# A residual graph network: counting loop by single chunks, input loaded tile by tile, mixing table made first

## The chip, the cores and the metric

The kernel runs on one core of a Trainium2 chip. The time is the device time of one execution in microseconds (us). The core has five engines with a program each: TensorE (PE, matmuls; its weight loads are shown as PEld), VectorE (DVE), ScalarE (ACT), GpSimd (POOL) and SyncE (SP, which here only issues DMAs). They wait for each other through semaphores. SPq and ACTq in the profile are the DMA issues of SP and ACT.

## The reference, cut to what matters

```python
x   = normal(1250, 512)
src, dst = [s, d, loop], [d, s, loop]     # 10000 random pairs both ways and 1250 self loops: 21250 edges, sorted by dst
x = layernorm(x + L0(x))   # GCN convolution with W (512x512), batch norm, gelu, residual
x = layernorm(x + L1(x))   # two SAGE layers: relu(h @ W_self + mean_of_neighbours(h) @ W_neigh + b)
x = layernorm(x + L2(x))   # two relational layers, two relations, weights mixed from 30 bases:
                           #   w[r] = sum_b att[r, b] * basis[b]          (30 x 512 x 512)
                           #   msg  = sigmoid(x_j @ gate_w[r]) * x_j @ w[r], r = edge_type; summed by row
x = layernorm(x + L3(x))   # x + neighbours' sum, relu(x @ W1 + b1) @ W2 + b2
```

All four layers use the same edges. So the kernel first turns the edge list into a matrix of counts (how many edges of each relation go from node s to node d) and then computes every sum over neighbours as a matrix product with it.

## The kernel before, in words

The change lies in the first stage, the counting stage, which runs until about 206 us. Afterwards come seven units (`UNITS`), each with a dense product for ten tiles of 128 nodes (`dense`) and a product with the counts (`agg`); nothing of them is touched.

**Counting.** The edges, sorted by dst, lie in `CHUNKS` = 170 chunks of 128. The 1280 padded nodes are cut into `NWIN` = 40 windows of 32 destination nodes. For each chunk that a window touches, VectorE writes two one-hot tables: `oh_lo` (128 columns: the low part of src) and `oh_key` (640 columns: destination within the window, relation, and tile of src), by two instructions (L1130 and L1132). TensorE multiplies them (L568, two matmuls of 320 columns for each chunk) and adds them up in PSUM, one matmul group for each window. ScalarE copies the sum to `B` (`window_out`, L758). Four windows make a node tile: TensorE turns its counts by products with the identity (`turn_counts`, L589, five groups in `COUNT_STEPS`), ScalarE copies them to `A` (L764), VectorE adds the two relations into `AT` (`sum_counts`, L1155), and TensorE counts degrees (L597).

Which chunks a window touches is found on the chip: VectorE takes the smallest and largest dst of each chunk (L1076), compares them with the windows' limits (L1079 to L1088), GpSimd takes the maximum over partitions (L510), and VectorE packs for each window the first chunk, the number of extra loop turns and their running sum into `tbl` (L1109 to L1123). The window's work goes by pairs of chunks: two fixed pairs, and between them a loop (`Fori`) of `more` turns with a pair each. Every window takes at least `LEAST` = 3 pairs, so the loop has at least one turn, and an odd number of chunks is rounded up. The tables lie in rings: `2 * FIXED` pairs for the fixed ones and `MORE` = 2 pairs for the loop's. VectorE may begin window w when TensorE has finished window w-2 (`wait(dve, s_win, w - 1)`).

**Mixing.** Beside this TensorE mixes the first relational layer's weights: 8 groups of 15 products in fp32 (L612), `mixT` (a table made by VectorE from att, L1092 to L1095) times a tile of 256 KB of the bases. Each is one "mix", and takes two rows of matmul in the profile. SP loads the tiles into 8 slots (`load_mix`); tile n waits until mix n-8 is done (`s_mx` at n-7). 15 mixes come ahead of window 0, the other 105 are spread behind the windows, two or three behind each (`SHARES`), in the order window, turned counts, mixes. ScalarE writes out each finished group (`mixed_out`).

**The input.** SP loads x behind the first 15 basis tiles, in a DMA of 2 MB (tiles 0 to 7, L465) and two small ones (L466, L468). VectorE takes the largest magnitude of x in five pieces (L1262, L1265), one each in front of windows 6 to 9 and the last in front of window 10, followed there by the maximum of the first weights (`most`, L1193) and `sum_counts`. GpSimd spreads the maximum over the partitions; behind window 12 VectorE makes the scale (`s_s0`). ScalarE then splits x into two fp16 halves tile by tile (`split_x`, L795 and L797) behind windows 17, 19, ... 35, and GpSimd computes the low half (L542).

## Time and profile before

| | us |
|---|---|
| time before, median of 3 runs | 944.89 (941.42 to 945.36) |
| the profiled execution | 940.41 |
| its span | 938.4 |
| TensorE busy in the span | 893.2 |
| VectorE busy | 681.1 |
| ScalarE busy | 280.8 |
| GpSimd busy | 86.1 |
| window 0 starts on TensorE | 21.71 |
| window 39 starts on TensorE | 200.99 |

The profile is one execution. Its times count from the span's start. "Busy" is the time in which an engine has an instruction in work; matmuls overlap in their records, so the distance from one start to the next is the rate, and a single record is longer than that. What stands in square brackets behind a row is how long the engine had been idle and what released it; "issue" there is a time in which the engine waited for nothing that the profile shows. The DMA columns give the busy share of the 16 DMA engines and GB/s. A row that merges several instructions shows their count behind x and the time from the first start to the last end.

### The profile page before, as it was taken

The numbers are of one execution on the slowest core, as the hardware profiler recorded it, in microseconds if no ns is written. First come the engines' busy times: TensorE is split into PE (matmuls) and PEld (weight loads), VectorE is DVE, ScalarE is ACT, GpSimd is POOL, SyncE is SP. The second block draws the span as 40 slices with busy tenths as digits, with TensorE's granted clock in tenths as the row PEclk, the third lists the DMA queues.
The fourth block names the chain that finished last, engine by engine and source line by source line (L and its number), as shares of the span: only waits on it lengthen the run. The fifth ranks groups of instructions, "written<-read, shape, count | busy, mean of one in ns | idle before, by whom it ended". The sixth has DMA issues, their size and how long they took to land.

```text
span 938.4 us, 13110 instructions
## 1 busy us (share of the span) xinstructions
PE 893.2 (95%) x4320; PEld 433.9 (46%) x4320; DVE 681.1 (73%) x1469; ACT 280.8 (30%) x431; POOL 86.1 (9%) x66
## 2 busy tenths in 40 slices
PE   6798999999996999999999899999999999999997
PEld 3354555554554544434444344444444444444443
DVE  7598998866997789798999888995324245552247
ACT  0132444443863313324132211113411131032321
POOL 1000011120321001202121000001300010010000
PEclk9899999999997999999999899999999999999999
DMA  8855556559544585788643765450031014322238
GB/s 261 275 163 157 157 182 181 171 136 232 159 147 135 144 239 177 191 248 176 182 120 97 168 147 171 124 127 12 22 79 34 1 54 115 90 66 46 39 66 229
DMA packets 134779, 129.53 MB, mean 138 GB/s; under 512 B 80575, under 2 KB 81044, under 8 KB 134714
## 3 DMA queue, kind: packets, MB, share of 16 engines
q10 hardware_dynamic: 96192, 60.25, 25.2%
q1 hardware_dynamic: 38522, 68.45, 25.0%
q8 instruction: 36, 0.59, 0.3%
q14 instruction: 29, 0.24, 0.1%
HBM read 97.80 MB, written 12.52 MB: 118 GB/s over the span
## 4 chain that ended last, share of the span: by engine, by line
PE 64%; DVE 17%; DMA 7%; ACT 4%; issue 3%; DVEq 1%; ACTq 1%; POOL 1%
PE Dp L658 24%; PE Dp L688 24%; PE T L612 9%; PE Dp L568 5%; DVE acc L1239 4%; DVE Zraw L1350 1%; DMA xr<-xres 1%; DVE stt L1331 1%; ACT W L1002 1%; DMA wst<-mixd 1%; DVE w L1368 1%; ACT wst L853 1%; DMA Zraw<-in_basis 1%; DMA stage<-in_basis 1%; POOL Zraw L525 1%
## 5 line engine op out<-in xcount | busy, mean ns | idle before, releaser
L658 PE MATMUL Dp<-W,hT 128*128 128x512 f16 x792 | 175.7, 381 | 3.6 <-DMA hT<-S 3.6
L688 PE MATMUL Dp<-Zraw,A 128*128 128x512 f16 x800 | 173.0, 379 | 0.0
L1239 DVE SCALAR_TENSOR_TENSOR acc<-stage,att,acc 128x512 f32<-128x512 f32 x232 | 163.7, 770 | 3.2 <-DMA stage<-in_basis 3.1
L688 PE MATMUL Dp<-Zraw,AT 128*128 128x512 f16 x600 | 130.0, 379 | 0.0
L658 PEld LDWEIGHTS Dp<-W,hT 128*128 128x128 f16 x792 | 77.7, 98 | 96.7 <-DMA hT<-S 3.8
L688 PEld LDWEIGHTS Dp<-Zraw,A 128*128 128x128 f16 x800 | 78.3, 98 | 94.4
L1132 DVE TENSOR_SCALAR Zraw<-hT,w 128x640 f16<-128x640 f16 (+1 forms) x240 | 114.4, 476 | 0.6 <-issue 0.4
L688 PEld LDWEIGHTS Dp<-Zraw,AT 128*128 128x128 f16 x600 | 58.7, 98 | 70.8
L1130 DVE TENSOR_SCALAR Zraw<-hT,w 128x128 f16<-128x128 f16 (+1 forms) x240 | 62.6, 261 | 24.8 <-PE Dp L568 15.9
L568 PE MATMUL Dp<-Zraw 128*128 128x320 f16 (+1 forms) x480 | 73.4, 300 | 3.3 <-DVE Zraw L1132 2.8
L1368 DVE SCALAR_TENSOR_TENSOR w<-Dp,aggc,S 128x512 f32<-128x512 f32 x40 | 29.9, 747 | 60.0 <-PE Dp L688 54.0
L954 ACT ACTIVATE Zraw<-Dp,zsc 128x512 f16<-128x512 f32 x46 | 29.4, 684 | 126.3 <-PE Dp L658 122.9
L612 PE MATMUL T<-stage,W 128*128 128x512 f32 x120 | 60.4, 626 | 7.2 <-DVE W L1095 7.2
L568 PEld LDWEIGHTS Dp<-Zraw 128*128 128x128 f16 (+1 forms) x480 | 46.7, 98 | 44.2 <-issue 27.7
L612 PE MATMUL T<-Zraw,W 128*128 128x512 f32 x120 | 58.4, 609 | 6.6 <-DMA Zraw<-in_basis 6.6
L1308 DVE SCALAR_TENSOR_TENSOR Zraw<-Dp,zsc,Zraw 128x512 f16<-128x512 f32 x26 | 19.5, 749 | 59.0 <-ACT Zraw L954 59.0
L525 POOL TENSOR_TENSOR W<-wst,W 128x1024 f16<-128x1024 f32 x18 | 43.1, 2415 | 159.7 <-ACT W L856 159.7
L993 ACT ACTIVATE w<-w,s_in 128x512 f32<-128x512 f32 x30 | 21.6, 720 | 120.5 <-DVE w L1368 115.5
L758 ACT ACTIVATE Zraw<-Dp 128x640 f16<-128x640 f32 x40 | 28.1, 701 | 97.6 <-PE Dp L568 95.5
L658 PE MATMUL Dp<-W,stage 128*128 128x512 f16 x240 | 52.8, 379 | 1.2 <-DVE Zraw L1308 1.2
L713 PE MATMUL Dp<-AT,Zraw 128*128 128x512 f16 (+1 forms) x240 | 43.4, 344 | 0.0
L658 PE MATMUL Dp<-W,wst 128*128 128x512 f16 x144 | 34.0, 401 | 4.9 <-DVE S L1316 4.9
(174 smaller groups left out, 913.7 us busy)
## 6 DMA issues: line engine op xcount, KB each, us to landing
stage<-in_basis SPq DMA_DIRECT2D x180, 256.0 KB, 2.9
Zraw<-in_basis SPq DMA_DIRECT2D x60, 256.0 KB, 2.8
xres<-w ACTq DMA_DIRECT2D x30, 256.0 KB, 2.4
xr<-xres ACTq DMA_DIRECT2D x30, 256.0 KB, 2.9
wst<-in_Wn ACTq DMA_DIRECT2D x4, 1024.0 KB, 5.5
wst<-in_Ws ACTq DMA_DIRECT2D x4, 1024.0 KB, 5.6
wst<-mixd ACTq DMA_DIRECT2D x4, 1024.0 KB, 5.9
wst<-in_root ACTq DMA_DIRECT2D x3, 1024.0 KB, 6.8
```

What stands on the lines that cost most here:

```text
L525: pool.tensor_tensor(weights_of(u, m)[:, 1, 2 * h:2 * h + 2, :], source, weights_of(u, m)[:, 0, 2 * h:2 * h + 2, :], ALU.subtract).then_in ...
L568: last = nc.tensor.matmul(Dp[:, j, b, 0:HALF], oh_lo[:, ds(slot * (2 * P) + q * P, P)], oh_key[:, ds(slot * (2 * KEYS) + (q * KEYS + b * H ...
L612: nc.tensor.matmul(T[:, 1, :], mixT[:, b * P:(b + 1) * P], mix_in[n % MIX_SLOTS], start=(b == 0), stop=(b == PAIRS - 1)).then_inc(s_mx, 1)
L658: last = nc.tensor.matmul(dense_bank(u, t, m), turned[:, hp, k * P:(k + 1) * P], weights_of(u, m)[:, wp, k, :], start=(n == 0), stop=(n == ...
L688: last = nc.tensor.matmul(sum_bank(t), a[:, k, ds(t * P, P)], Z[:, r, h, k, :], start=(n == 0), stop=(n == count - 1))
L713: last = nc.tensor.matmul(Df[:, j, c:c + w], Z[:, 0, h, k, b * P:(b + 1) * P], AT[:, k, c:c + w], start=(k == 0 and h == 0), stop=(k == NT ...
L758: nc.scalar.activation(B[:, t % 2, :, :, a:a + WIN].rearrange("p s r (b d) -> p b (s r) d", b=2), Dp[:, w % 2, 0:2, 0:HALF].rearrange("p b ...
L954: nc.scalar.activation(Z[:, r, 0, ds(t, 1), :], dense_rows(u, t, r), ACT.Copy, scale=scale).then_inc(s_zhi[u], 1)
L1130: v.tensor_scalar(oh_lo[:, ds(slot * (2 * P) + q * P, P)], iota_n[:, 0:P], lo_f[:, ds(c + q, 1)], None, ALU.is_equal)
L1132: last = v.tensor_scalar(oh_key[:, ds(slot * (2 * KEYS) + q * KEYS, KEYS)], iota_n, wkey[:, w:w + 1], key_f[:, ds(c + q, 1)], ALU.add, ALU ...
L1239: last = v.scalar_tensor_tensor(part, stage[:, q, :], a, part, ALU.mult, ALU.add)
L1368: v.scalar_tensor_tensor(w1[:, j:j + 1, :], sum_bank(t).rearrange("p (a d) -> p a d", a=1), c, rest, ALU.mult, ALU.add).then_inc(s_pre[u], 1)
```

## The change

- **Loop by single chunks.** `LEAST` is now 5 chunks, and the loop between the fixed pairs takes one chunk each turn (`chunk_of` on VectorE, `chunk_product` on TensorE). A window takes as many chunks as it touches, at least five. The loop's ring holds `MORE` = 4 single chunks, the same memory as two pairs. The table of windows no longer rounds to even numbers.
- **Input tile by tile.** x is loaded in ten DMAs of one tile, each behind three basis tiles of mixing groups 1 and 2.
- **Maximum later.** VectorE waits for all of x in front of window 10; the pieces of the maximum stand in front of windows 10 to 14, the scale behind window 17, and ScalarE splits x behind windows 19, 21, ... 37.
- **Mixing table first.** The first part of `mixT` is made right behind the two reductions over dst, ahead of the range operations; the second part behind them.

```diff
@@ -18,8 +18,8 @@
-MORE = 2
-LEAST = 3
+MORE = 4
+LEAST = 2 * FIXED + 1
...
@@ -428,8 +428,8 @@
-        XS_FROM = 4
-        Z_SCALED = 40
+        XS_FROM = 19
+        Z_SCALED = 38
...
@@ -462,13 +462,19 @@
             sp.dma_start(typ_i, typ_t).then_inc(e_edge, 16)
             sp.dma_start(src_i, src_t).then_inc(e_edge, 16)
             load_mix(0, MIX_FIRST)
-            sp.dma_start(acc_x, x[0:XA * P, :].rearrange("(t p) d -> p t d", p=P)).then_inc(e_x, 16)
-            sp.dma_start(xr[:, 0, :], x[XA * P:(NT - 1) * P, :]).then_inc(e_x, 16)
-            sp.wait_ge(s_pad, 1)
-            sp.dma_start(xr[0:LAST, 1, :], x[(NT - 1) * P:N, :]).then_inc(e_x, 16)
+
+            def load_x(t):
+                rows = min(P, N - t * P)
+                if rows < P:
+                    sp.wait_ge(s_pad, 1)
+                sp.dma_start(x_in(t)[0:rows, :], x[t * P:t * P + rows, :]).then_inc(e_x, 16)
+
+            for t in range(NT):
+                load_mix(1 + t // 5, 3 * (t % 5), 3 * (t % 5) + 3)
+                load_x(t)
             for tile, vec in ((b0T, b0), (gamT, gamma), (betT, beta)):
                 sp.dma_start(tile[:, :], vec).then_inc(s_bn, 16)
-            for mix_group in range(1, GROUPS):
+            for mix_group in range(3, GROUPS):
                 load_mix(mix_group)
             sp.dma_start(att[:, :, :].rearrange("p r b -> p (r b)"),
                          att2.rearrange("(a r) b -> a (r b)", a=1).broadcast_to([P, REL * BASES])).then_inc(s_att, 16)
...
@@ -561,14 +567,17 @@
         @block.tensor
         def _(pe):
 
-            def pair_product(slot, j, start=False, stop=False):
-
-                for q in range(2):
-                    for b in range(2):
-                        last = nc.tensor.matmul(Dp[:, j, b, 0:HALF], oh_lo[:, ds(slot * (2 * P) + q * P, P)],
-                                                oh_key[:, ds(slot * (2 * KEYS) + (q * KEYS + b * HALF), HALF)],
-                                                start=start and q == 0, stop=stop and q == 1)
+            def chunk_product(slot, j, start=False, stop=False):
+
+                for b in range(2):
+                    last = nc.tensor.matmul(Dp[:, j, b, 0:HALF], oh_lo[:, ds(slot * P, P)],
+                                            oh_key[:, ds(slot * KEYS + b * HALF, HALF)], start=start, stop=stop)
                 return last
+
+            def pair_product(pair, j, start=False, stop=False):
+
+                chunk_product(2 * pair, j, start=start)
+                return chunk_product(2 * pair + 1, j, stop=stop)
 
             def window(w, j):
                 _, more, base = window_range(pe, w)
...
@@ -577,7 +586,7 @@
                 pair_product(FIXED * (w % 2), j, start=True)
                 with pe.Fori(0, more) as i:
                     pe.wait_ge(s_more, base + i + 1)
-                    pair_product(pe.snap(((base + i) & (MORE - 1)) + OH), j).then_inc(s_moreu, 1)
+                    chunk_product(pe.snap(((base + i) & (MORE - 1)) + 2 * OH), j).then_inc(s_moreu, 1)
                 pe.wait_ge(s_oh, FIXED * (w + 1))
                 pair_product(FIXED * (w % 2) + 1, j, stop=True).then_inc(s_win, 1)
 
...
@@ -783,8 +792,10 @@
                             turned_out(t - 1, g, count_bank(t - 1, g))
                     for g in range(groups_done(w - 1) if w else 1, groups_done(w)):
                         mixed_out(g)
-                    first = (t - XS_FROM) * 2 + i // 2
-                    if i % 2 and 0 <= first < NT:
+                    first, odd = divmod(w - XS_FROM, 2)
+                    if first == 0 and not odd:
+                        act.wait_ge(s_s0, 1)
+                    if not odd and 0 <= first < NT:
                         split_x(first)
                     if w == NWIN - 2:
                         turn_to(2, 0)
...
@@ -1075,7 +1084,19 @@
             dve.wait_ge(e_row, 16)
             v.tensor_reduce(mnx[0:HC, 0:2], dstr[0:HC, :, :], AX.X, ALU.min)
             link(v.tensor_reduce(mnx[0:HC, 2:4], dstr[0:HC, :, :], AX.X, ALU.max))
-            dve.wait_ge(s_const, 5)
+            dve.wait_ge(e_att, 32)
+            dve.wait_ge(s_const, 8)
+            v.tensor_tensor(eye, ident[:, 0:P // 2], ident[:, P // 2:P], ALU.add).then_inc(s_eye, 1)
+            dve.wait_ge(s_eye, 1)
+
+            def mix_table(a0, a1):
+
+                v.tensor_tensor(mixT[:, a0 * P // 2:a1 * P // 2].rearrange("p (a i) -> p a i", a=a1 - a0),
+                                eye.rearrange("p (a i) -> p a i", a=1).broadcast_to([P, a1 - a0, P // 2]),
+                                attp[:, a0:a1].rearrange("p (a i) -> p a i", i=1).broadcast_to([P, a1 - a0, P // 2]),
+                                ALU.mult).then_inc(s_mixT, 1)
+
+            mix_table(0, 2 * MIX_FIRST)
             for g in range(2):
                 link(v.tensor_scalar(fl[0:HC, 0:NWIN], wlo[0:HC, :], mnx[0:HC, 2 + g:3 + g], None, ALU.is_le))
                 link(v.scalar_tensor_tensor(fl[0:HC, NWIN:2 * NWIN], whi[0:HC, :], mnx[0:HC, g:g + 1],
...
@@ -1087,15 +1108,7 @@
-            dve.wait_ge(e_att, 32)
-            dve.wait_ge(s_const, 8)
-            v.tensor_tensor(eye, ident[:, 0:P // 2], ident[:, P // 2:P], ALU.add).then_inc(s_eye, 1)
-            dve.wait_ge(s_eye, 1)
-            for a0, a1 in ((0, 2 * MIX_FIRST), (2 * MIX_FIRST, BASES)):
-                v.tensor_tensor(mixT[:, a0 * P // 2:a1 * P // 2].rearrange("p (a i) -> p a i", a=a1 - a0),
-                                eye.rearrange("p (a i) -> p a i", a=1).broadcast_to([P, a1 - a0, P // 2]),
-                                attp[:, a0:a1].rearrange("p (a i) -> p a i", i=1).broadcast_to([P, a1 - a0, P // 2]),
-                                ALU.mult).then_inc(s_mixT, 1)
+            mix_table(2 * MIX_FIRST, BASES)
...
@@ -1107,11 +1120,9 @@
-            link(v.tensor_scalar(w_st, w_st, float(CHUNKS - 2 * LEAST), None, ALU.min))
+            link(v.tensor_scalar(w_st, w_st, float(CHUNKS - LEAST), None, ALU.min))
-            link(v.tensor_scalar(w_n, w_n, float(2 * LEAST), 1.0, ALU.max, ALU.add))
-            link(v.tensor_scalar(w_n, w_n, 0x1FE, None, ALU.bitwise_and))
-            link(v.tensor_scalar(w_p, w_n, 0.5, -float(FIXED), ALU.mult, ALU.add))
+            link(v.tensor_scalar(w_p, w_n, float(LEAST), -2.0 * FIXED, ALU.max, ALU.add))
...
@@ -1124,14 +1135,16 @@
+            def chunk_of(w, slot, c):
+                v.tensor_scalar(oh_lo[:, ds(slot * P, P)], iota_n[:, 0:P], lo_f[:, ds(c, 1)], None, ALU.is_equal)
+                return v.tensor_scalar(oh_key[:, ds(slot * KEYS, KEYS)], iota_n,
+                                       wkey[:, w:w + 1], key_f[:, ds(c, 1)], ALU.add, ALU.is_equal)
+            def pair_of(w, pair, c):
+                chunk_of(w, 2 * pair, c)
+                return chunk_of(w, 2 * pair + 1, c + 1)
...
@@ -1140,11 +1153,11 @@
                     wait(dve, s_win, w - 1)
                     pair_of(w, FIXED * (w % 2), first).then_inc(s_oh, 1)
                     with dve.Fori(0, more) as i:
-                        c = nc.s_assert_within(dve.snap(first + i * 2 + 2 * FIXED), 0, CHUNKS - 2,
+                        c = nc.s_assert_within(dve.snap(first + i + 2 * FIXED), 0, CHUNKS - 1,
                                                skip_runtime_bounds_check_because=ends)
                         n = dve.snap(base + i)
                         dve.wait_ge(s_moreu, n + 1)
-                        pair_of(w, dve.snap((n & (MORE - 1)) + OH), c).then_inc(s_more, 1)
+                        chunk_of(w, dve.snap((n & (MORE - 1)) + 2 * OH), c).then_inc(s_more, 1)
                     pair_of(w, FIXED * (w % 2) + 1, nc.s_assert_within(dve.snap(first + 2), 0, CHUNKS - 2,
                                                                        skip_runtime_bounds_check_because=ends)).then_inc(s_oh, 1)
 
...
@@ -1256,18 +1269,18 @@
             for u in (1, 3, 5):
                 v.memset(s_in[:, u:u + 1], LN_SCALE)
                 link(v.memset(i_in[:, u:u + 1], 1.0 / LN_SCALE))
-            windows_to(6)
-            dve.wait_ge(e_x, 48)
+            windows_to(10)
+            dve.wait_ge(e_x, 16 * NT)
             for piece in range(4):
                 v.tensor_reduce(xcol[:, piece:piece + 1], acc_x[:, 2 * piece:2 * piece + 2, :].rearrange("p t d -> p (t d)"), AX.X,
                                 ALU.max, apply_absolute_value=True).then_inc(s_xc, 1)
-                windows_to(7 + piece)
+                windows_to(11 + piece)
             v.tensor_reduce(xcol[:, 4:5], xr[:, :, :].rearrange("p a d -> p (a d)"), AX.X, ALU.max,
                             apply_absolute_value=True).then_inc(s_xc, 1)
             dve.wait_ge(s_xc, 5)
             v.tensor_reduce(xin[:, :], xcol[:, :], AX.X, ALU.max).then_inc(s_xin, 1)
             weight_work("counts", 0, 0)
-            windows_to(13)
+            windows_to(18)
             dve.wait_ge(s_xmax, 1)
             power_scale(s_in[:, 0:1], i_in[:, 0:1], xmax[:, :])
             v.nop().then_inc(s_s0, 1)
```

On VectorE, at the start of the program, these rows stand before (w and hT hold the small tables of ranges, W holds `mixT`):

```order
L1076 TENSOR_REDUCE w<-hT 85x2
L1077 TENSOR_REDUCE w<-hT 85x2
L1080 TENSOR_SCALAR hT<-hT,w 85x40
L1081 SCALAR_TENSOR_TENSOR hT<-hT,w 85x40
L1085 SCALAR_TENSOR_TENSOR w<-hT,w 85x40 x2
L1080 TENSOR_SCALAR hT<-hT,w 85x40
L1081 SCALAR_TENSOR_TENSOR hT<-hT,w 85x40
L1085 SCALAR_TENSOR_TENSOR w<-hT,w 85x40 x2
L1092 TENSOR_TENSOR hT<-ident 128x64
L1095 TENSOR_TENSOR W<-hT,sd_att 128x384
L1095 TENSOR_TENSOR W<-hT,sd_att 128x1536
```

and these after:

```order
L1085 TENSOR_REDUCE w<-hT 85x2
L1086 TENSOR_REDUCE w<-hT 85x2
L1089 TENSOR_TENSOR hT<-ident 128x64
L1094 TENSOR_TENSOR W<-hT,sd_att 128x384
L1101 TENSOR_SCALAR hT<-hT,w 85x40
L1102 SCALAR_TENSOR_TENSOR hT<-hT,w 85x40
L1106 SCALAR_TENSOR_TENSOR w<-hT,w 85x40 x2
L1101 TENSOR_SCALAR hT<-hT,w 85x40
L1102 SCALAR_TENSOR_TENSOR hT<-hT,w 85x40
L1106 SCALAR_TENSOR_TENSOR w<-hT,w 85x40 x2
L1094 TENSOR_TENSOR W<-hT,sd_att 128x1536
```

The table's first part (128x384, three mixes' worth) has moved ahead of the range operations; the larger second part stands behind them in both.

On SP, the queue that issues the loads, this is the place where x stands (stage and Zraw are the basis slots, acc and xr the tiles of x), as a difference:

```order
+L470 DMA acc<-in_x 128x512
+L458 DMA stage<-in_basis 128x512 x2
+L458 DMA Zraw<-in_basis 128x512
+L470 DMA acc<-in_x 128x512
 L458 DMA Zraw<-in_basis 128x512 x3
-L465 DMA acc<-in_x 128x8x512
-L466 DMA xr<-in_x 128x512
-L468 DMA xr<-in_x 98x512
-L470 DMA b0T<-in_b 128x4
-L470 DMA gamT<-in_gamma 128x4
-L470 DMA betT<-in_beta 128x4
+L470 DMA acc<-in_x 128x512
```

The three loads of x have left their place behind basis tile 14; a tile of x now follows three basis tiles each time, down to the last one behind basis tile 44.

## Rows read from the trace of the kernel before

**Rows 1.** The page: TensorE's busy time, share of the span, instructions.

```profile
PE   893.2 (95%) x4320; PEld 433.9 (46%) x4320; DVE 681.1 (73%) x1469; ACT 280.8 (30%) x431; POOL 86.1 (9%) x66
```

**Rows 2.** Busy time by stretch: stretch, its length, then each engine; clock; DMA.

```profile
5.00:15.00 10.00, 7.85 (x15) 3.57 (x16) 8.23 (x35) 0.00 (x0) 0.81 (x4) 1.00 0.95 310
92.00:190.00 98.00, 97.94 (x565) 56.71 (x566) 89.41 (x290) 45.61 (x76) 11.91 (x10) 1.00 0.59 177
```

**Rows 3.** Who waited for whom, first 300 us: total us, times, longest.

```profile
DVE Zraw L1130 <- PE Dp L568: 15.9, 8, 9.0
```

**Rows 4.** Timeline, first 17 us: start, duration, engine, line, operation, operands, idle before.

```profile
2.39 1.53 SPq L458 DMA_DIRECT2D stage<-in_basis  x3
...
4.07 0.24 DVE L1080 TENSOR_SCALAR hT<-hT,w 85x40 f32<-85x40 f32 x1
...
6.54 2.23 DVE L1095 TENSOR_TENSOR W<-hT,sd_att 128x384 f32<-128x384 f16 x2
...
7.15 5.28 PE L612 MATMUL T<-stage,W 128*128 128x512 f32 x8 [7.15 <-DVE W L1095]
...
16.90 0.26 DVE L1130 TENSOR_SCALAR Zraw<-hT,w 128x128 f16 x1 [0.43 <-issue]
```

**Rows 5.** DMAs: landing of basis tile 0; of tiles at 10-60 us; x issue.

```profile
DMA to landing us min/median/max: 3.0/3.0/3.0
...
DMA to landing us min/median/max: 2.7/3.0/12.1
...
15.41 0.43 SPq L465 DMA_DIRECT2D acc<-in_x  x1
```

**Rows 6.** Timeline of TensorE, windows 0, 1 and 3 with the mixes behind.

```profile
21.71 1.79 PE L568 MATMUL Dp<-Zraw 128*128 128x320 f16 x12
...
30.14 2.05 PE L612 MATMUL T<-Zraw,W 128*128 128x512 f32 x2 [6.64 <-DMA Zraw<-in_basis]
...
33.69 2.08 PE L568 MATMUL Dp<-Zraw 128*128 128x320 f16 x12
...
41.53 1.79 PE L568 MATMUL Dp<-Zraw 128*128 128x320 f16 x12
43.16 1.88 PE L612 MATMUL T<-Zraw,W 128*128 128x512 f32 x4
44.87 1.02 PE L612 MATMUL T<-stage,W 128*128 128x512 f32 x2
```

**Rows 7.** Timeline of TensorE: starts of windows 9, 10, 11, 13, 15, 17, 19.

```profile
66.08 1.79 PE L568 MATMUL Dp<-Zraw 128*128 128x320 f16 x12
72.38 0.70 PE L568 MATMUL Dp<-Zraw 128*128 128x320 f16 x4 [1.43 <-DVE Zraw L1132]
...
77.34 1.79 PE L568 MATMUL Dp<-Zraw 128*128 128x320 f16 x12
...
85.45 0.71 PE L568 MATMUL Dp<-Zraw 128*128 128x320 f16 x4
...
95.61 1.79 PE L568 MATMUL Dp<-Zraw 128*128 128x320 f16 x12
...
103.72 1.79 PE L568 MATMUL Dp<-Zraw 128*128 128x320 f16 x12
...
112.33 1.79 PE L568 MATMUL Dp<-Zraw 128*128 128x320 f16 x12
```

**Rows 8.** Timeline of VectorE: window 8, then the maxima and sums before window 10.

```profile
58.36 0.24 DVE L1130 TENSOR_SCALAR Zraw<-hT,w 128x128 f16<-128x128 f16 x1
...
61.47 1.21 DVE L1262 TENSOR_REDUCE xcol<-acc 128x1 f32<-128x1024 f32 x1
...
65.71 1.21 DVE L1265 TENSOR_REDUCE xcol<-xr 128x1 f32<-128x1024 f32 x1
...
69.41 0.82 DVE L1155 TENSOR_TENSOR AT<-Zraw 128x1280 f16<-128x1280 f16 x1
...
71.11 0.25 DVE L1130 TENSOR_SCALAR Zraw<-hT,w 128x128 f16<-128x128 f16 x1 [0.63 <-issue]
```

21 lines of the change are left out of this document (6 added, 15 removed).

## The prediction

> **What bounds the kernel now.** I began with the page: TensorE is busy for 95% of a span of 938.4 us [rows 1], so a change pays only where it shortens TensorE's row of work or fills a hole in it. The edit lies in the counting stage, so I next cut the span into stretches. From 92 to 190 us TensorE is busy for 97.94 of 98.00 us at a granted clock of 1.00, while VectorE has 89.41 and the DMA engines are 59% busy [rows 2]. In its steady part the counting stage is TensorE's. The waits agree: VectorE stood for 15.9 us behind TensorE, eight times [rows 3]. Then I read TensorE's timeline for what is not steady: its first matmul at 7.15 us [rows 4], one hole of 6.64 us at 30.14 us, put down to a basis tile's DMA [rows 6], and windows that last longer than others of their kind [rows 7].
>
> The stage ends for TensorE with window 39 (201 us) and its three mixes, near 206 us; everything later waits for these results, in an order that the diff leaves alone. So I price the edits on this stage and take the difference through to the end.
>
> **Prices.** A window of six chunks starts at 41.53 and the next work at 43.16 [rows 6]: 1.63 us for 12 matmuls, 0.272 us for a chunk. Two mixes take 44.87 - 43.16 = 1.71 us, 0.857 each; a mix counts as two matmuls in the rows. Windows 17 and 18 run without a wait, 103.72 to 112.33 [rows 7]: 8.61 us for two windows, five mixes, three turned groups and the degrees. Groups and degrees cost what is left, 8.61 - 2 x 1.63 - 5 x 0.857 = 1.07, so 0.53 for each window. On VectorE six chunks take 61.47 - 58.36 = 3.11 us, 0.52 each, and a maximum of two x tiles 1.2 us [rows 8].
>
> **1. One chunk per loop turn.** A window holds 21250/40 = 531 edges, 4.15 chunks of 128, so it touches five or six. Working the ranges out with the reference's own dst gives 31 windows of five and 9 of six; before, all 40 take six. That removes 31 chunks: 31 x 0.272 = 8.4 us of TensorE, all on the path. VectorE is rid of 31 x 0.52 = 16.1 us, off the path in the steady part. Nine windows go round the loop twice, which no window of before does. The loop's entry and exit lie inside the 1.63 us already, so I take the second turn at 0. Its other end: VectorE stood 0.43 us at its first entry into the loop (16.47 to 16.90) [rows 4], and nine of those on TensorE would be 3.9 us. Below nothing it can't go, since it only adds instructions.
>
> **2. The x load in pieces.** Before, 2.5 MB of x go in front of basis tile 15 [rows 5]. TensorE could mix tile 15 at 21.71 + 1.63 = 23.34 and be at window 1 two mixes later, at 25.06; it is there at 33.69 [rows 6]. Lost: 8.6 us. Now one x tile of 256 KB follows every three basis tiles, and tile 15 is issued when eight mixes are done, about 14 us. Windows with 2.5 mixes each then need 2.5 x 4/3 = 3.3 tiles in some 4.0 us, 0.85 MB or 213 GB/s, with the first weights (1 MB) on top for a while. The queue moved 310 GB/s at 5 to 15 us, with only tiles of this size and the edge lists in it [rows 2]. So the hole goes: -8.6 us. Its bound on the other side is under the rivals.
>
> Those 310 GB/s are 91% of what a 1 MB transfer gets in a table of the Trainium skill (DMA: Bandwidth & Descriptors, Measured): 341 GB/s, against 138 for 64 KB, with the advice to batch DMAs to 1 MiB or more. That rule speaks against cutting a 2 MB load into eight. By it x would need an estimated 2.5/0.138 = 18 us instead of 2.5/0.341 = 7.3, at worst 11 us more of queue time. The row bears it out little: small DMAs in a row overlap.
>
> **3. Mixing table first.** VectorE makes the table's first part after the eight range operations (4.07 to about 6.1 us), at 6.54, and TensorE starts at 7.15 [rows 4]. With the table right behind the two reductions VectorE comes to it at 4.07; a short first step and the 0.61 us from 6.54 to 7.15 bring that to about 4.9. But basis tile 0, issued at 2.39, lands 3.0 us later [rows 4, 5], at 5.4. So TensorE starts at 5.45: -1.7 us. The next tiles come at some 0.85 us each and are taken at 0.857. If they come late the gain is 0. The range operations, and with them the table of windows, come 0.8 us later, but TensorE is in its 15 mixes until 19.6 us; nothing waits.
>
> **4. The maximum taken later.** The waits of before first. Windows 9 and 10 start at 66.08 and 72.38, window 11 at 77.34: 11.26 us for a pair that takes 8.61 elsewhere (17 and 18 have the same groups and mixes); 2.65 us lost, because VectorE has 71.11 - 65.71 = 5.40 us of maxima and sums in front of window 10 [rows 7, 8]. Windows 13 and 14 take 95.61 - 85.45 = 10.16 instead of 8.61: 1.55 lost [rows 7]. These 4.2 us go.
>
> New waits take their place, and here the edit pays back a third. VectorE now waits for all ten x tiles in front of window 10. The tenth stands behind basis tile 44, which waits for the 37th mix; that mix ends with window 8, so just when window 9 starts (call it 0). Two issues of 0.43 us and 3.0 us of landing [rows 5]: 3.9. Then queued on VectorE: one maximum (1.2, to 5.1), sum_counts with the table load (71.11 - 69.41 = 1.70, to 6.8) [rows 8], and five chunks (2.6, to 9.4). TensorE's last pair of chunks takes 0.54 more, so it ends window 10 at 10.0. Undisturbed it would start window 10 at 4.5 (1.36 + 0.53 + 2.57) and end it at 5.8. Lost: 4.2 us. Window 11 has six chunks behind another maximum and ends 0.4 late. By window 13 VectorE and TensorE are level (VectorE has made it at 21.0, TensorE ends it at 21.7). In front of window 14 stands the same string of 5.40 us that stood before window 10, then five chunks: 21.0 + 5.4 + 2.6 = 29.0, TensorE ends it at 29.6, undisturbed 21.7 + 0.53 + 2.57 + 1.36 = 26.2. Lost: 3.4 us. New waits: 4.2 + 0.4 + 3.4 = 8.0 us. Their ends: 0, if VectorE had enough lead, and 16, if the last x tile lands 8 to 9 us later (the longest landing is 12.1 us [rows 5]).
>
> The split of x moves two windows later (17 to 35, now 19 to 37), two windows before TensorE needs its results; I take 0.
>
> **Sum.** -8.4 - 8.6 - 1.7 - 4.2 + 8.0 = -14.9 us. The profiled execution took 940.4 us, of which 938.4 are the span; it becomes 925.5. That execution lies under all three timed runs (941.42 to 945.36, median 944.89); from the median the sum gives 930.0. A small rest speaks for a little more gain: the two mixes behind the hole ran at a slower clock (2.05 us for one [rows 6]). I forecast **929 us**.
>
> **Rivals.**
> A. *The new waits don't arise.* The last x tile would have to be there when VectorE comes, or VectorE two windows ahead through both places. For it: VectorE has 16 us less to do. Against it: it can't be more than two windows ahead, and the DMA's place behind the 37th mix is fixed. Gain 14.9 + 8.0 = 22.9: 921 to 922 us.
> B. *The new waits are twice as long*, the last x tile landing late while weights and mixed results move too. For it: the 12.1 us landing. Loss 16 in place of 8.0, perhaps with 2 us from loop turns: 937 us.
> C. *The range doesn't fit or the gains are given back.* If VectorE, not TensorE, set the period, 31 chunks less on TensorE would bring nothing; [rows 2, 3] speak against it. Or the second turn costs 3.9 us and the start gains nothing: together with B about 943.
> D. *Slower: the basis tiles starve.* Eight slots are in flight, and every three basis tiles carry an x tile behind them. With a landing time L, 30 mixes need 30 x 4/3 x L/8 = 5L us if slots are always waited for. Where TensorE would need about 50 us for this stretch (window 0 to 11), the other gains are used up from 5L = 66, L = 13.2 us. At L = 15 it is 75 us: nine more than before, 954 us. One landing of 12.1 us is in the rows, with 2.5 MB in front; the median is 3.0 [rows 5].
>
> **Chances.** Forecast 0.66, A 0.14, B 0.13, C 0.05, D 0.02. A measurement of this kernel tells about 0.5% (4.7 us) from no change. Faster by more: the forecast, A and nearly all of B, 0.93; within it: most of C and a rest of B, 0.05; slower: D, 0.02. Range 918 to 938: it takes in A at 921, less 3 for the runs' spread, and B at 937. The forecast's own range is 924 to 934.
>
> **What would show it.** (1) 418 chunk matmuls instead of 480, at 1.36 us for most windows, and none of the nine longer windows more than 0.3 us over 1.63. (2) No hole behind window 0; window 1 starts near 22.8, and the granted clock is 1.00 from 20 to 40 us. (3) First matmul at 5.3 to 5.6 us. (4) VectorE waits for a DMA into the x tiles in front of window 10, TensorE then waits for VectorE by about 4 us, and again by 3 to 4 us in front of window 14. (5) The first dense matmul of unit 0 starts near 191, not 206, and all later distances are as before. It is wrong if TensorE has no waits at windows 10 and 14 (A), or waits for basis tiles between windows 1 and 9 (D), or if the stage gets shorter and a later one longer.

## The result and the profile after

The changed kernel takes 932.5 us in the median of 4 runs (930.7 to 935.52), the kernel before 943.15 in 4 runs beside it (940.66 to 945.36). The ratio is 0.9901 with a 95% interval of 0.9876 to 0.9926: faster, by 9.3 us by the ratio (7.0 to 11.7 by its interval) and 10.7 by the medians. The forecast was 929 us with a range of 918 to 938. The range held the time and the sign was right; the forecast gain of 14.9 us was about half again too large. The profiled execution of after took 935.5 us (span 933.7), the slowest of its four, so the 4.7 us between the two spans are less than the medians differ by. I account for the counting stage, which the edit changes.

The page of after, against [rows 1]:

```profile
PE 888.9 (95%) x4258; PEld 428.9 (46%) x4258; DVE 668.8 (72%) x1405; ACT 280.8 (30%) x431; POOL 85.5 (9%) x66
...
L573 PE MATMUL Dp<-Zraw 128*128 128x320 f16 (+1 forms) x418 | 67.1, 307 | 9.2 <-DVE Zraw L1141 9.1
```

TensorE lost the 62 matmuls of 31 chunks, and a wait of 9.1 us for VectorE stands where there were 2.8. The stretches, against [rows 2]; the third is the one that had the hole:

```profile
5.00:15.00 10.00, 9.08 (x15) 3.94 (x16) 9.09 (x36) 0.00 (x0) 0.81 (x4) 1.00 0.94 324
92.00:190.00 98.00, 96.63 (x544) 54.41 (x544) 84.00 (x262) 48.97 (x80) 13.32 (x11) 1.00 0.59 173
...
20.00:40.00 20.00, 20.00 (x90) 10.71 (x89) 15.75 (x60) 4.61 (x7) 0.00 (x0) 1.00 0.97 343
```

From 20 to 40 us TensorE is busy without a gap. From 92 to 190, where it had 0.06 us idle before, it has 1.37. The waits of the first 220 us, against [rows 3]:

```profile
DVE Zraw L1140 <- issue: 15.7, 37, 1.2
PE Dp L573 <- DVE Zraw L1141: 9.1, 6, 3.6
...
DVE xcol L1275 <- DMA xr<-in_x: 6.7, 1, 6.7
...
DVE Zraw L1140 <- PE Dp L573: 4.7, 6, 1.5
```

The balance has turned: VectorE waits 4.7 us for TensorE (15.9 before), TensorE 9.1 for VectorE. TensorE's timeline, against [rows 4, 6, 7] (the start, windows 0 to 2, then windows 9, 10, 11, 13, 14 and 15; the view ends within window 15, so its row counts 11 of the 12 matmuls):

```profile
5.92 6.58 PE L621 MATMUL T<-stage,W 128*128 128x512 f32 x8 [5.92 <-DMA stage<-in_basis]
12.34 3.60 PE L621 MATMUL T<-Zraw,W 128*128 128x512 f32 x8
...
21.78 1.52 PE L573 MATMUL Dp<-Zraw 128*128 128x320 f16 x10
...
24.86 1.52 PE L573 MATMUL Dp<-Zraw 128*128 128x320 f16 x10
...
28.79 1.52 PE L573 MATMUL Dp<-Zraw 128*128 128x320 f16 x10
...
55.06 1.52 PE L573 MATMUL Dp<-Zraw 128*128 128x320 f16 x10
...
63.25 2.93 PE L573 MATMUL Dp<-Zraw 128*128 128x320 f16 x10 [3.59 <-DVE Zraw L1141]
...
68.46 1.92 PE L573 MATMUL Dp<-Zraw 128*128 128x320 f16 x12
...
76.43 1.52 PE L573 MATMUL Dp<-Zraw 128*128 128x320 f16 x10
...
83.30 2.93 PE L573 MATMUL Dp<-Zraw 128*128 128x320 f16 x10 [2.27 <-DVE Zraw L1141]
...
88.61 1.66 PE L573 MATMUL Dp<-Zraw 128*128 128x320 f16 x11
```

The hole is gone (window 0 to window 1: 3.08 us, before 11.98). TensorE starts earlier, but its first eight matmuls last 6.42 us to the next group, and window 0 starts no earlier than before. Windows 10 and 14 start late, and their ten matmuls take 2.93 us instead of 1.52: TensorE gets chunks at VectorE's pace, and its own is slower behind the idle time (see step 4). VectorE in front of window 10, against [rows 8]:

```profile
59.13 1.22 DVE L1275 TENSOR_REDUCE xcol<-acc 128x1 f32<-128x1024 f32 x1 [6.72 <-DMA xr<-in_x]
60.27 0.82 DVE L1168 TENSOR_TENSOR AT<-Zraw 128x1280 f16<-128x1280 f16 x1
...
61.98 0.25 DVE L1140 TENSOR_SCALAR Zraw<-hT,w 128x128 f16<-128x128 f16 x1 [0.64 <-issue]
```

VectorE had been done since 52.4 us and stood 6.7 us for the last x tile; only then came the maximum, the sum of the counts (`sum_counts`) and the chunks. The first dense matmul of unit 0 comes at 197.88 us (before 206.37): the stage is 8.5 us shorter. By windows (start to start, after less before, each a sum of the timeline's distances):

| stretch | forecast | measured |
| --- | --- | --- |
| start to window 0 | -1.7 | +0.1 |
| window 0 (the hole, one chunk) | -8.9 | -8.9 |
| windows 1 to 8 | -1.9 | -2.2 |
| windows 9 to 14 | +2.4 | +4.0 |
| windows 15 to 37 | -4.4 | -2.3 |
| windows 38 and 39 | -0.5 | +0.8 |
| sum | -14.9 | -8.5 |

The 6.4 us that are missing lie in four places: the start 1.8 (most of it this one profile's, as the third experiment shows), windows 9 to 14 1.6, windows 15 to 37 2.0, the last two 1.3; windows 1 to 8 gave 0.3 more than forecast. After the stage the distances of the two profiles differ by 3.8 us (732.0 and 735.8). The gap of the profiles is no measure of the edit there: kernels whose code there is the same gave 732 to 739 us for this part.

### The profile page after: what moved, and what is told of

The parts are those of the page before. It is cut to its first block, busy times and chain, and to the rows that moved or that the text cites. A ratio compares the mean times of both kernels' runs of the same rounds, so it can differ in the third digit from the quotient of the medians.

```text
span 933.7 us, 12912 instructions
## 1 busy us (share of the span) xinstructions
PE 888.9 (95%) x4258; PEld 428.9 (46%) x4258; DVE 668.8 (72%) x1405; ACT 280.8 (30%) x431; POOL 85.5 (9%) x66
## 4 chain that ended last, share of the span: by engine, by line
PE 61%; DVE 18%; DMA 7%; issue 5%; ACT 4%; DVEq 3%; POOL 1%; ACTq 0%; SPq 0%
PE Dp L667 25%; PE Dp L697 24%; PE T L621 6%; DVE acc L1252 4%; DMA stage<-in_basis 3%; PE Dp L573 3%; DVE Zraw L1141 2%; DMA wst<-mixd 2%; DVE Zraw L1140 1%; DVE Zraw L1363 1%; ACT W L1011 1%; PE T L667 1%; DVEq L1140 1%; ACT wst L864 1%; DVE w L1381 1%
## 5 line engine op out<-in xcount | busy, mean ns | idle before, releaser
L1141 DVE TENSOR_SCALAR Zraw<-hT,w 128x640 f16<-128x640 f16 (+1 forms) x209 | 96.4, 461 | 0.8 <-issue 0.7
L573 PE MATMUL Dp<-Zraw 128*128 128x320 f16 (+1 forms) x418 | 67.1, 307 | 9.2 <-DVE Zraw L1141 9.1
L1140 DVE TENSOR_SCALAR Zraw<-hT,w 128x128 f16<-128x128 f16 (+1 forms) x209 | 59.3, 284 | 22.1 <-issue 15.7
L573 PEld LDWEIGHTS Dp<-Zraw 128*128 128x128 f16 (+1 forms) x418 | 40.5, 99 | 48.8 <-issue 30.1
L531 POOL TENSOR_TENSOR W<-wst,W 128x1024 f16<-128x1024 f32 x18 | 42.9, 2400 | 158.2 <-ACT W L867 158.2
L963 ACT ACTIVATE Zraw<-Dp 128x512 f16<-128x512 f32 x26 | 15.5, 596 | 74.9 <-PE Dp L667 72.3
```

The lines of the kernel that those rows point to most:

```text
L531: pool.tensor_tensor(weights_of(u, m)[:, 1, 2 * h:2 * h + 2, :], source, weights_of(u, m)[:, 0, 2 * h:2 * h + 2, :], ALU.subtract).then_in ...
L573: last = nc.tensor.matmul(Dp[:, j, b, 0:HALF], oh_lo[:, ds(slot * P, P)], oh_key[:, ds(slot * KEYS + b * HALF, HALF)], start=start, stop=stop)
L963: nc.scalar.activation(Z[:, r, 0, ds(t, 1), :], dense_rows(u, t, r), ACT.Copy, scale=scale).then_inc(s_zhi[u], 1)
L1140: v.tensor_scalar(oh_lo[:, ds(slot * P, P)], iota_n[:, 0:P], lo_f[:, ds(c, 1)], None, ALU.is_equal)
L1141: return v.tensor_scalar(oh_key[:, ds(slot * KEYS, KEYS)], iota_n, wkey[:, w:w + 1], key_f[:, ds(c, 1)], ALU.add, ALU.is_equal)
```

## The experiments

Twelve kernels ran. Each ratio is to the kernel before on the same chip (medians 941.5 to 942.2 us in the four series), with its 95% interval. "Stage" is from the start of window 0 to the first dense matmul of unit 0: 184.7 us before, 176.1 after.

**The three parts alone.** Each is the kernel before with one part of the diff: the loop of single chunks; x in pieces and its maxima later; the mixing table first.

> The kernel before with the single-chunk loop alone; x stays one 2 MB load, maxima in front of windows 6 to 10. Theory T1 (a loop turn with one chunk costs VectorE more than its 0.52 us: in the changed kernel a window of five chunks took VectorE 3.07 us instead of 2.6, one of six with two turns 4.3 to 4.7 instead of 3.31): VectorE's windows show the same 3.07 and 4.3 to 4.7 us here, TensorE still gains on 31 windows, and the time is 5 to 8 us below before. Rival T2 (the lost gain comes only from VectorE having lost its lead in front of window 10, the loop costs nothing): VectorE's windows are 2.8 and 3.3 us and the time is 8.4 us or more below before.

Measured: 937.3 us, 0.9954 (0.9931 to 0.9977); stage 178.8. VectorE's undisturbed windows are those of T1: 3.07 us for five chunks, 4.34 for six (window 11). The gain, 4.3 us by the ratio and 5.0 by the medians, lies at the lower end of T1's 5 to 8 or just under it, and T2's 8.4 is out.

> The kernel before with the tile-by-tile load of x, the later maxima and the later split alone. Both theories: the hole behind window 0 goes (8.6 us), the old waits at windows 10, 13 and 14 (4.2 us) go, new ones come in front of windows 10 and 14. T1: these are as long as in the changed kernel less what its loop adds, 8 to 9 us together, so the stage ends 3 to 5 us earlier than before. T2 (the lead is lost because x comes late): the same, and in addition later windows wait for VectorE as in the changed kernel (windows 18 to 24 and 39).

Measured: 944.0 us, 1.0027 (1.0005 to 1.0050); stage 183.7. The hole was gone and nothing was won; the stage is 1.0 us shorter, where the expectation had 3 to 5 for both theories, and none of the windows 18 to 24 lost anything, against T2. TensorE at window 10, and VectorE's wait, in this kernel:

```profile
65.70 3.64 PE L574 MATMUL Dp<-Zraw 128*128 128x320 f16 x12 [3.67 <-DVE Zraw L1138]
```

```profile
DVE xcol L1268 <- DMA xr<-in_x: 7.2, 1, 7.2
DVE Zraw L1136 <- PE Dp L574: 7.1, 8, 1.3
```

Windows 9 and 10 lost 6.9 us against their undisturbed 8.61, windows 13 and 14 4.3, where before the two places lost 4.2 in all; the last two windows took 1.0 longer. Together that is 8.0 of the 8.6 us of the hole.

> The kernel before with the mixing table first alone. Forecast of the prediction: first matmul 1.7 us earlier and window 0 as much earlier. Theory C (TensorE starts earlier but stays at the slow clock for longer, as in the changed kernel, where weight loads of the first mixes stood 0.85 us apart until 11.9 us instead of 10.2): first matmul near 5.9 us, window 0 at 21.4 to 21.8, no gain. Rival: the basis tiles come too late; then the weight loads have idle times put down to a DMA in front of them.

Measured: 941.5 us, 0.9997 (0.9979 to 1.0015). TensorE started at 5.51 us, window 0 at 21.33 (before 21.71).

```profile
5.51 6.54 PE L612 MATMUL T<-stage,W 128*128 128x512 f32 x8 [5.51 <-DVE W L1085]
11.89 3.60 PE L612 MATMUL T<-Zraw,W 128*128 128x512 f32 x8
```

A start 1.64 us earlier leaves 0.38 at the second group. The way from the first matmul to window 0 varies by itself, from 14.6 to 15.9 us. Over all profiles window 0 starts at 22.2 us in the mean where the table comes late (6 kernels, 21.71 to 22.87) and at 20.9 where it comes first (8 kernels, 20.14 to 21.78): 1.3 us, which is within this run's interval. The expectation's slower first matmuls are there; what they are is the last point of this document.

**Parts one and two together.**

> Parts 1 and 2 of the change (one chunk per loop turn; x in pieces with its maxima later), the mixing table where it was. Theory (part 2 pays only with part 1: the hole behind window 0 was also the time in which VectorE caught up, and part 1 makes VectorE's windows 0.24 us shorter): about as the changed kernel plus the 0 to 1 us of the earlier start, 932 to 935 us. Rival (the parts add: ratios 0.9954 and 1.0027 alone): 0.998 of the kernel before, 940 to 942 us; then the third part would carry the difference.

Measured: 935.3 us, 0.9922 (0.9893 to 0.9952). The parts do not add: 0.9954 x 1.0027 would be 0.998, outside the interval. In the counting stage they nearly do: 5.9 and 1.0 us alone, 8.4 together (stage 176.3). The rest of the difference lies behind the stage, where no part changes the code, and no run tells why. The third part stands for the rest, 2.8 us by the medians, with intervals that overlap.

**Every window with two loop turns.** The changed kernel with the least number of chunks raised by one, so that 31 windows get back a sixth chunk, now as a second turn:

```diff
-LEAST = 2 * FIXED + 1
+LEAST = 2 * FIXED + 2
```

> The changed kernel with LEAST = 6 chunks: every window takes six chunks and two loop turns, as many chunks as before. T1: VectorE needs 4.3 to 4.7 us for each window and 1.7 more for every fourth, about 4.8 a window against TensorE's 4.4, so VectorE sets the counting stage: TensorE waits for it in most windows and the stage is 15 to 25 us longer than in the changed kernel, longer than before. T2: only the 8.4 us of TensorE's 31 chunks come back, the time is near 941.

Measured: 964.6 us, 1.0248 (1.0229 to 1.0267). The waits of the stage:

```profile
DVE Zraw L1140 <- issue: 27.4, 57, 1.2
PE Dp L573 <- DVE Zraw L1141: 19.9, 26, 3.0
```

31 more chunks cost 32 us where TensorE needs 0.27 each, 8.4 in all. The stage is 30.5 us longer than in the changed kernel, more than T1's 15 to 25. Windows 38 and 39 alone take 16.98 us in place of 10.84, since GpSimd holds VectorE up there (last section); the rest of the stage takes 24.3 us more, 0.8 for each of its 29 new chunks. TensorE waits 26 times, but not everywhere: windows 24, 27 and 28, for instance, take the 4.48 us that they took before. The price is in the changed kernel's own rows, VectorE's window 5:

```profile
34.13 0.25 DVE L1140 TENSOR_SCALAR Zraw<-hT,w 128x128 f16<-128x128 f16 x1 [0.16 <-issue]
...
35.30 0.25 DVE L1140 TENSOR_SCALAR Zraw<-hT,w 128x128 f16 x1
35.50 0.45 DVE L1141 TENSOR_SCALAR Zraw<-hT,w 128x640 f16 x1
36.57 0.25 DVE L1140 TENSOR_SCALAR Zraw<-hT,w 128x128 f16 x1 [0.62 <-issue]
```

From the first turn's chunk to the second's are 1.27 us, not 0.52. Without other work and waits a window of six chunks takes 4.33 us on VectorE (window 15), of five 3.07, and before, with two chunks in one turn, six took 3.31.

**The x load earlier.** The changed kernel with an x tile behind every two basis tiles:

```diff
-                load_mix(1 + t // 5, 3 * (t % 5), 3 * (t % 5) + 3)
+                for n in (2 * t, 2 * t + 1):
+                    load_mix(1 + n // PAIRS, n % PAIRS, n % PAIRS + 1)
                 load_x(t)
...
+            load_mix(2, 5)
```

> The changed kernel, but one x tile follows every two basis tiles instead of every three, so the tenth stands behind basis tile 19 (which waits for the 12th mix) and not behind tile 44 (the 37th mix). Theory (VectorE has no lead to spare, and what is put in its way is lost on TensorE): VectorE's wait of 6.7 us for the last x tile goes; without it the maximum starts near 52.4 us instead of 59.1 and the chunks of window 10 are ready before TensorE comes, so the 5.3 us lost at windows 9 and 10 go; VectorE reaches windows 13 and 14 with two windows of lead, and of the 4.1 us lost there 1 to 4 go too. Stage 6 to 9 us shorter: 924 to 927 us. Rival (only the late transfer matters): windows 9 and 10 lose nothing, windows 13 and 14 lose their 4.1 us as before: 927 to 928 us. Second rival (VectorE's whole work sets the stage, the place of the transfer does not matter; the waits come back further on): 931 to 933 us, as the changed kernel.

The expectation names a wrong place: the tiles are counted from tile 15 on, so the tenth x tile stands behind basis tile 34, which waits for the 27th mix, and was issued at 38.81 us (after: 55.63). Measured: 925.8 us, 0.9828 (0.9787 to 0.9869), the best version by the medians; stage 169.3. TensorE's windows 9, 10 and 11, and the wait in window 14:

```profile
54.16 1.52 PE L575 MATMUL Dp<-Zraw 128*128 128x320 f16 x10
58.59 1.52 PE L575 MATMUL Dp<-Zraw 128*128 128x320 f16 x10
62.23 1.79 PE L575 MATMUL Dp<-Zraw 128*128 128x320 f16 x12
...
75.59 0.70 PE L575 MATMUL Dp<-Zraw 128*128 128x320 f16 x4 [0.92 <-DVE Zraw L1143]
```

Windows 9 and 10 take 8.07 us, undisturbed, where the changed kernel needs 13.40; windows 13 and 14 take 10.03 in place of 12.18 (8.08 undisturbed). The theory's 924 to 927 held. The first rival falls by the windows (13 and 14 did not lose their 4.1 us again), the second by the time: the wait for the last tile was worth 5.3 us at window 10, and 2.2 us at window 14 by the lead that VectorE keeps.

**The x load early and the maxima earlier.** As the last one, with the maxima at windows 6 to 10 and the weights' maximum behind window 16:

```diff
-            windows_to(10)
+            windows_to(6)
             dve.wait_ge(e_x, 16 * NT)
...
-                windows_to(11 + piece)
+                windows_to(7 + piece)
...
+            windows_to(17)
             weight_work("counts", 0, 0)
```

> The changed kernel with the x tiles behind every two basis tiles, the five maxima of x in front of windows 6 to 10 instead of 10 to 14, and the maximum of the first weights (2.3 us) in front of window 17 by itself. In windows 1 to 9 TensorE has 2.5 mixes in each (4.0 us) where VectorE needs 3.07, so a maximum of 1.2 us fits there nearly for nothing. Theory (no lead): the 5.3 us at windows 9 and 10 and the 4.1 us at 13 and 14 both go, and windows 16 to 18 lose at most 1 us: 922 to 925 us. Rival (what counts is the sum of VectorE's work in the stage, wherever it stands): 930 to 933 us.

Measured: 934.5 us, 0.9914 (0.9887 to 0.9941): 8 to 9 us worse than the last, and my 922 to 925 was wrong. The rival's 930 to 933 is nearer to the number, but does not have the cause. By the misplaced tile above x was not there yet; the wait and most of the loss moved with the maximum (windows 5 and 6 lost 8.3 us, and windows 17 and 18, behind the weights' maximum, 2.9), here VectorE, then TensorE at window 6:

```profile
43.88 1.22 DVE L1277 TENSOR_REDUCE xcol<-acc 128x1 f32<-128x1024 f32 x1 [6.92 <-DMA xr<-in_x]
```

```profile
48.02 2.93 PE L575 MATMUL Dp<-Zraw 128*128 128x320 f16 x10 [5.33 <-DVE Zraw L1143]
```

The same two edits (x tiles, maxima) on the kernel before with part two:

> The kernel before (two chunks per loop turn) with part 2 alone, but with the x tiles behind every two basis tiles, the maxima in front of windows 6 to 10 and the weights' maximum in front of window 17. Part 2 alone gave 944.0 us against 942.2: it filled the hole of 6.6 us and lost as much at windows 9, 10, 13, 14 and 39. Theory (it was lost to VectorE's wait for the last x tile and to the two strings of its other work): most of the 8.6 us of the hole now shows: 935 to 938 us. Rival (VectorE's work of six chunks a window, 3.11 us, leaves no room without the hole, wherever the maxima stand): 941 to 944 us.

Measured: 943.1 us, 0.9996 (0.9972 to 1.0021), with the same wait of 6.9 us. It can't tell the two theories apart, since x came late in it; the next one does.

**Part two alone with x earlier,** the maxima at windows 10 to 14:

> The kernel before (two chunks per loop turn) with part 2, but an x tile behind every two basis tiles, so that the tenth stands behind basis tile 34 (it waits for the 27th mix), not behind tile 44; the maxima of x stay in front of windows 10 to 14. This is part 2 without its wait for the last x tile. Theory (part 2 alone gained nothing because VectorE stood 7.2 us for that tile): of the 8.6 us of the hole at least 5 show, and the strings in front of windows 10 and 14 may cost 1 to 3 us: 935 to 938 us. Rival (VectorE has no lead without the hole, whenever x lands, since its six chunks take 3.3 us a window): 941 to 944 us.

Measured: 937.0 us, 0.9947 (0.9926 to 0.9968); stage 176.6, 8.0 us shorter than before. So the hole is worth its 8 us in the stage as soon as VectorE doesn't stand for x, with two chunks in a turn as well. The rival, that VectorE needs the hole for its lead, falls: windows 9 and 10 lost nothing, and windows 13 and 14 lost 4.1 us, as much as before lost at both places (4.2). Of the 8 us, 4.5 show in the time. In this profile the part behind the stage was 4.5 us longer (736.6 against 732.0); 2.2 of them lie between the first product of unit 0 with the counts and the start of the matmuls of L731 (47.3 us became 49.5), and the last section tells where.

**An x tile behind every basis tile,** then the same with the maxima at windows 6 to 10 and the weights' maximum in front of window 13 (`windows_to(13)` for the 17 above):

```diff
-                load_mix(1 + t // 5, 3 * (t % 5), 3 * (t % 5) + 3)
+                load_mix(1, t, t + 1)
                 load_x(t)
...
+            load_mix(1, NT)
+            load_mix(2)
```

> The changed kernel, but one x tile behind every single basis tile from tile 15 on: the tenth stands behind basis tile 24 (it waits for the 17th mix) and is issued in window 2. Maxima in front of windows 10 to 14. Theory (the basis tiles have slots to spare, as with one x tile behind every two): the same 925 us, 923 to 928. Rival (with as many bytes of x as of basis tiles in the queue the basis tiles come late): TensorE waits for basis tiles at windows 1 to 4, up to 5 us in all: 927 to 931 us.

> The kernel of one x tile behind every basis tile, with the maxima of x in front of windows 6 to 10 and the maximum of the first weights in front of window 13. In the earlier attempt at this the last x tile came 6.9 us after VectorE had reached the maximum at window 6, and the kernel took 934.5 us. Here the tile is issued some 10 us earlier. Theory (a VectorE job costs nothing in the windows that carry 2.5 mixes, and what was lost was the wait for the tile): no wait for x in front of window 6, nothing lost at windows 6 to 10, at most 1 us at window 13: 922 to 926 us. Rival (the order of VectorE's jobs costs it as such): 930 us or more.

Measured: 928.2 us, 0.9855 (0.9829 to 0.9881), and 928.3 us, 0.9856 (0.9832 to 0.9880). Now basis tiles come late, in the first of the two:

```profile
31.59 2.21 PE L623 MATMUL T<-Zraw,W 128*128 128x512 f32 x4
35.13 1.12 PE L623 MATMUL T<-stage,W 128*128 128x512 f32 x2 [1.33 <-DMA stage<-in_basis]
```

Window 3 takes 5.86 us instead of 3.93 (7.01 in the second). That is rival D's mechanism in small, and the rival of the first expectation. In the second kernel the wait for x in front of window 6 is down to 0.5 us and windows 6 to 12 lose nothing; its time is 2 us over the 922 to 926 I gave; window 3 alone lost 3.1 us to the basis tiles. By the medians two basis tiles to one x tile is the best of the three mixtures; against one to one the intervals overlap.

**GpSimd's subtraction cut short.** The best version, where GpSimd computes only 16 of 512 columns of the first weights' low half and ScalarE writes zeros into the rest:

```diff
+                    part = slice(0, 16 if u == 0 else D)
...
+                    if u == 0:
+                        nc.scalar.activation(weights_of(u, m)[:, 1, 2 * h:2 * h + 2, 16:D], source[h][:, :, 16:D], ACT.Copy, scale=0.0)
```

> The kernel with an x tile behind every two basis tiles (925.8 us), with GpSimd's two subtractions of the first weights' low half (2.14 us each, at 180.6 to 184.9 us) cut to 16 of 512 columns; the other columns of the low half are left out (ScalarE writes zeros there). Theory (a GpSimd subtraction over SBUF holds VectorE's comparison up until it ends: the two at 180.6 and 182.8 us took 2.30 and 2.11 us in place of 0.44 and 0.25, and TensorE then waited 1.91 us at window 39): these two are back at 0.5 us or less, TensorE's wait in window 39 goes, windows 38 and 39 together last 8.5 us instead of 10.8, and the first dense matmul comes 2 us earlier: 923 to 924.5 us. Rival (the two run side by side by chance, and TensorE waits for VectorE there since VectorE is late anyway): the wait stays, 925 to 927 us.

Measured: 927.1 us, 0.9837 (0.9810 to 0.9863): no gain in time. In the stage it did what was expected where it was expected: windows 38 and 39 take 8.75 us (10.83). But ScalarE, with the zeros to write, now came 1.4 us late to a turned group, and window 37 took 5.98 us instead of 4.44. The edit did a second thing: by the same zeros the subtraction of the last x tile came 1.2 us later (180.66 us in place of 179.47) and met no comparison either, as VectorE was through by then. So this run takes all of GpSimd's work away from window 39 and not the two subtractions alone. That such a subtraction holds VectorE up rests on the rows of the last section too, and what it is worth in the whole time is not shown.

## Why the prediction came out as it did

**Step 1, single chunks.** Right for TensorE: 418 chunk matmuls, 1.36 us for a window of five. The step failed in its last sentence on VectorE. It took the second turn at nothing, with 3.9 us as the worst, and counted VectorE rid of 31 x 0.52 = 16.1 us. Measured, a window of five saves 0.24 us (3.31 to 3.07), an estimated 7.4 for 31 of them; a window of six costs 1.0 us more, in eight of nine windows, 8.2. By this estimate VectorE is rid of nothing. The bound of 3.9 us was meant for TensorE, and the sum charged VectorE with no price for a turn. It shows in windows 18 and 19, behind VectorE's input scales (0.6 and 0.4 us over the forecast; the kernel with part two alone loses nothing there), and in part in window 26 (1.0): all of the 2.0 us of windows 15 to 37. In window 26 a second thing meets it. VectorE comes there from the two-turn windows 24 and 25, and GpSimd, subtracting for the split of x, holds up one comparison of 0.25 us before it (1.23 us at 129.10) and one within it:

```profile
135.03 1.19 POOL L548 TENSOR_TENSOR S<-w,S 128x512 f16<-128x512 f32 x1 [4.76 <-ACT S L808]
```

```profile
135.13 1.15 DVE L1140 TENSOR_SCALAR Zraw<-hT,w 128x128 f16<-128x128 f16 x1
```

TensorE waits 0.82 us behind it. With part two alone the same subtractions cost window 26 nothing, so it takes both.

**Step 2, the hole.** Right in size: -8.9 us with one chunk, and the clock stayed at 1.00. It was also right that x in small pieces costs nothing here: the DMA engines moved 343 GB/s from 20 to 40 us, where before, with the 2 MB transfer of x in it, they had 320 (a 1 MB load of weights lies in both stretches). The Trainium skill (DMA: Bandwidth & Descriptors, Measured) advises to batch DMAs to 1 MiB or more. In this trace 256 KB tiles issued one behind the other moved no fewer bytes in the same time. VectorE stood for 9.0 us in the hole, and one may think that it came out with a lead that is now missing. The kernel with part two and x earlier speaks against it: there the filled hole showed its 8 us.

**Step 3, mixing table first.** First matmul at 5.92 us, 0.5 later than said, for the basis tile (5.34 to 5.51 in the seven other kernels with the table first, as forecast); and the mixes behind it were not at 0.857 each, but at 1.6 for the first four tiles, where before they were at 1.3, so that this profile gained nothing. The mean over the profiles is -1.3 against -1.7 forecast: the step is right within what can be told, and in this profile it was undone by the scatter of the start, which I had not allowed for.

**Step 4, the waits.** Places and order were right: VectorE for x, TensorE at window 10, again at 14. The landing was forecast 3.9 us behind window 9's start and was 4.1. The sizes were 5.3 and 4.1 us, not 4.2 and 3.4. TensorE ended window 10 at 10.9 us on that count, not 10.0. VectorE had its chunks at 9.7 instead of 9.4, and TensorE needed 1.2 us behind the last of them instead of 0.54, for its clock had fallen behind the idle time: its matmuls stood 0.27 us apart there, 0.14 in undisturbed windows, and the granted clock is 0.78 over 59 to 66 us:

```profile
59.00:66.00 7.00, 3.41 (x13) 1.24 (x12) 6.14 (x15) 0.00 (x0) 0.00 (x0) 0.78 0.38 111
```

**The split of x, taken at 0.** The last two windows cost 1.3 us more than forecast, and the term that failed is this one. GpSimd works in order: the subtraction for the tenth x tile (L548), then the two of the first weights' low half (L531). ScalarE now splits that tile behind window 37 and not 35, and the weights wait behind it, though ScalarE had their high half ready at 182.8 us. Before, then after:

```profile
190.92 4.21 POOL L525 TENSOR_TENSOR W<-wst,W 128x1024 f16<-128x1024 f32 x2 [1.84 <-ACT W L856]
```

```profile
187.19 1.15 POOL L548 TENSOR_TENSOR S<-w,S 128x512 f16<-128x512 f32 x1 [7.13 <-ACT S L808]
188.31 4.28 POOL L531 TENSOR_TENSOR W<-wst,W 128x1024 f16<-128x1024 f32 x2
```

Before, they began 10 us ahead of window 39, now 2.4, and while they last VectorE hardly gets on with this window's tables (last section). Windows 38 and 39 take 10.03 us before and 9.41 with part one alone; with part two 11.01 alone and 10.84 in the changed kernel.

**The rivals.** A is refuted, the waits came. B did not come: the new waits were 9.4 us, not 16, and its 937 us is 4.5 over the time. D did not come in the changed kernel; it came in the two with more x between the basis tiles. C said that VectorE, not TensorE, would set the period, and I put it aside by [rows 2, 3]. C as a whole is not true of the changed kernel, most of whose windows go at TensorE's pace, but putting it aside is the error that matters. The rows showed VectorE at 89.41 of 98 us, 9% of slack, and the price of a turn, which is no busy time, was not in them. The two-turn kernel comes nearest to C.

**The signs.** Chunk matmuls, the gone hole and the waits in front of windows 10 and 14 came as listed. Not so: window 19 took 2.03 us for its chunks, 0.4 over 1.63 where 0.3 was the most; window 1 started at 24.86 us, not 22.8, most of it for the slow start; the first dense matmul at 197.88, not 191. The time lies inside the forecast's range because together they cost 6.4 us and the range left 9 us above 929.

## What to carry to other kernels

When a loop turn is halved, price the turn on every engine that runs the loop, and multiply by the windows that go round twice; a saved unit is worth its full time only if no other cost comes with it. When a hole in the bounding engine is filled and the time stays, look first for the wait that the same edit put somewhere else. A job that moves later takes with it what its engine does behind it in order, so look where that now falls. When a consumer of a load is moved later, look for where the load's last piece is issued: here its place in the queue was worth 6.7 us by the medians, about two thirds of the gain of the whole change.
